# Three sage layers of a graph network put into one block, with the own products issued two tiles ahead

## The chip, the cores and the metric

One Trainium2 chip, one core. The metric is the device time of one execution in microseconds. The kernel before: 2948.05 us, the median of 3 runs (2944.01 to 2951.98).

## What is computed

A stack of four graph layers over 10000 nodes of 512 features and 2500 edges sorted by target, with a pre-norm and a residual around each. The change touches the second one, three "sage" steps in a row (h starts as the layer norm of x, with a relu):

```python
for l in range(3):
    h_neigh = segment_sum(h[src], dst) / maximum(deg, 1)
    rst = h @ W_self[l] + h_neigh @ W_neigh[l] + b[l]
    rst = relu(rst)
    h = rst / maximum(sqrt(sum(rst * rst, axis=-1)), 1e-12)
x = x + h
```

## The kernel before, in words

Nodes live in 79 tiles of 128 rows (NT). They are permuted so that every node which receives an edge lies in the last 20 tiles, the **zone**, tiles 59 to 78 (FT = 59, ET = 20). A sage layer so has an own product (h @ W_self) for every tile, and a neighbour product for the zone's alone. Each f32 product is made of three f16 products of high and low halves: `product` (L211) issues 4 chunks x 3 = 12 matmuls of 128x512. The halves of h, transposed, stay in SBUF (`slots16`) and are overwritten tile by tile with those of the next layer.

`gnn_program` calls `sage_layer(l)` (L1342) three times (L2542). Each call opens a block of its own: five instruction streams that all end before the next block's begin. Weights (`w`, 1 MB), bias and neighbour weights (`wn`) are loaded at the block's start (L1417 to L1419); TensorE and VectorE wait for weights and bias together (`s_w` at 32, L1582 and L1490).

Within a block every engine runs `pipeline` (L87): for step t = 0, 1, ... it emits the listed stages in order, each for tile t - lag; stages named in `edges` for edge tile t - lag. Steps below 12 and from 48 on are written out, those between are a hardware loop over four tiles. The engine streams are in order, so a wait holds all that stands behind it.

TensorE (L1604): `project` (L1584) does the own product of tile t into one of four PSUM banks `ps_z` (waiting for `s_r`, so that the bank of tile t-4 has been read) and, in the zone, the neighbour product on top of it, from `aT`, once `sums.s_lo` says that the edge tile's halves are there. In layer 2 `turn` (L1599) follows with lag 4: it transposes the normalised rows `h3` into one of two banks `ps_t`, waits for `s_turned` (h3 of that tile written) and for `s_lo` >= v.t - 1 (the low half of tile v-2 taken out of the same bank). Last comes `edge_sums`, lag FT - 2: eight 128x128 f32 matmuls of gathered rows and a selection matrix (L1316).

VectorE: `z_sum` (L1492, instruction at L1500) takes z out of PSUM, scaled and with the bias; `length` (L1508) the sum of squares, `clamp` (L1515) its lower bound; `lo_rows` (L1526) or in layer 2 `lo` (L1520) the low half; `residual` (L1533), `stats` (L719) and `aggregate` (L727) belong to layer 2's norm. Edge work: `sums.add` (L1254, L1259), `sums.lo` (L1338), and in layer 0 `sums.moments`. The order in layer 2 (L1541): residual(t-2), z_sum(t), edge_add, stats(t-2), length(t), lo(t-5), clamp(t), aggregate(t-2), edge_lo.

GpSimd: `factor` (L1461), the power -0.5; the norm's factors (L733 to L741); `gather` (L1292), an indirect DMA of an edge tile's source rows into one of two buffers `m`, lag FT - 3, once `sums.lo` has freed the buffer. ScalarE: `unit_rows` (L1571), `hi_rows` (L1559) or `hi` (L1552), `normed` (L1561, instruction at L746), `edge_hi` (L1332), in layer 0 also the norm of the gathered rows (L746). `normed` writes one of two buffers `h3` and waits until the store of tile v-2 has landed.

SP issues the DMAs: `edge_load` first (lag FT - 3: selection matrix L1281 once the sum of edge e-2 is done, carry weights L1240 once its `add` is), then in layers 0 and 1 `store` (L1435, lag 2) and the DMA transpose `turn` (L1439, lag 3); in layer 2 `store_x2` (L1430, lag 3), `store` (L1435, lag 5), `load_x` (L1425, lag 1).

```python
    def turn(v):
        pe.wait_ge(s_turned, v.t + 1)
        wait_count(pe, s_lo, v.t - 1)
...
    def normed(v):
...
        wait_count(act, s_turn, v.t + 1 - nh)
        wait_count(act, h_out[b], 16 * v.uses(nh))
```

Of the kernel before, what the change touches and what calls it, by code (L numbers as in the profile page):

```python
# [5 lines left out]
P = 128  # L6
# [10 lines left out]
C = D // P  # L17
# [32 lines left out]
LOOP_END = 48  # L50

# [58 lines left out]
def gnn_program(nc, x, src, dst, edge_attr, Wc, bc, Wlin, blin, Wself, Wneigh, bsage, W1, b1, W2, b2,  # L110
# [1115 lines left out]

    class Carry:


        def __init__(self, ctx, phase, n=2):  # L1230
            self.n = n
            self.w0 = [sb(ctx, f"{phase}_w0{b}", [P, P]) for b in range(n)]
            self.on = [sb(ctx, f"{phase}_on{b}", [P, C]) for b in range(2)]
            self.s_zero, self.s_added, self.s_on = sems(phase, "zero added on")
            self.w0_in = pair(phase, "w0in", n)

        def load(self, sp, t, kind):
            b = t.buf(self.n)
            wait_count(sp, self.s_added, t.t + 1 - self.n)
# [3 lines left out]
        def clear(self, dve, *others):  # L1243
            for ap in others:
                nc.vector.memset(ap, 0.0)
            nc.vector.memset(self.on[1][:, :], 0.0).then_inc(self.s_zero, 1)
# [15 lines left out]
    class EdgeSums:  # L1262


        def __init__(self, ctx, phase, source, kind, scale, nm, aT, ps_a, normed=False, nsel=2):
            self.source, self.kind, self.scale, self.aT, self.ps_a = source, kind, scale, aT, ps_a
            self.nm, self.nsel = nm, nsel
            self.m = [sb(ctx, f"{phase}_m{b}", [P, D]) for b in range(nm)]
            self.sl = [sb(ctx, f"{phase}_sel{b}", [P, P]) for b in range(nsel)]
            self.s_sum, self.s_hi, self.s_lo = sems(phase, "sum ahi alo")  # L1270
            self.m_in, self.sel_in = pair(phase, "min", nm), pair(phase, "selin", nsel)
            self.carry = Carry(ctx, f"{phase}_carry", nsel)
# [3 lines left out]
        def load(self, sp, e):  # L1276
            b = e.buf(self.nsel)
            if e.t < self.nsel:
                sp.wait_ge(self.carry.s_zero, 1)
# [6 lines left out]
        def clear(self, dve, *halves):  # L1286
            self.carry.clear(dve, *halves, *(sl[0:1, :] for sl in self.sl))
# [19 lines left out]
        def sums(self, pe, e):  # L1307
# [5 lines left out]
            pe.wait_ge(self.sel_in[e.buf(self.nsel)], 16 * (e.uses(self.nsel) + 1))  # L1313
            wait_count(pe, self.carry.s_added, e.t)
# [27 lines left out]
    def sage_layer(l):  # L1342

        final = l == 2
        phase = f"s{l}"
        scale_in = SCALE_LN if l == 0 else SCALE_UNIT
        scale_out = SCALE_LN if final else SCALE_UNIT
        unit = f"self{l}"
        with ExitStack() as ctx:
            w = sb(ctx, f"{phase}_w", [P, 2 * cols[unit]], F16)  # L1350
            wn = sb(ctx, f"{phase}_wn", [P, 2 * cols[unit]], F16)
            bias = sb(ctx, f"{phase}_bias", [P, D])
# [1230 lines left out]
```

## Time and profile before

| | |
|---|---|
| median of 3 runs | 2948.05 us |
| the profiled execution | 2975.29 us |
| its span, first to last instruction | 2973.6 us |
| mean granted clock of TensorE | 0.949 |
| sage layers: first own product to last neighbour product | 614.1 to 1586.7 us |

The profiled execution is 27 us above the median, and 1.7 us of it lie outside of its span. In rows of the trace, a start is in us from the beginning of the span, "x12" counts merged instructions, and "[1.2 <-ACT ...]" is the engine's idle time just before and what ended it. PE is TensorE's matmuls, PEld its weight loads, DVE VectorE, ACT ScalarE, POOL GpSimd, SPq the DMA issues of SP. A 128x512 matmul is shown as 379 ns long but the next starts about 215 ns after it, since they are pipelined.

### The profile page before, as it was taken

The numbers are of one execution on the slowest core, as the hardware profiler recorded it, in microseconds if no ns is written. First come the engines' busy times: TensorE is split into PE (matmuls) and PEld (weight loads), VectorE is DVE, ScalarE is ACT, GpSimd is POOL, SyncE is SP. The second block draws the span as 40 slices with busy tenths as digits, with TensorE's granted clock in tenths as the row PEclk, the third lists the DMA queues.
The fourth block names the chain that finished last, engine by engine and source line by source line (L and its number), as shares of the span: only waits on it lengthen the run. The fifth ranks groups of instructions, "written<-read, shape, count | busy, mean of one in ns | idle before, by whom it ended". The sixth has DMA issues, their size and how long they took to land. (4 is left out here: it accounts for less than half of the span.)

```text
span 2973.6 us, 45046 instructions
## 1 busy us (share of the span) xinstructions
PE 2450.1 (82%) x13328; PEld 1425.9 (48%) x13328; DVE 1950.1 (66%) x4623; ACT 1531.0 (51%) x2250; POOL 1195.6 (40%) x1984
## 2 busy tenths in 40 slices
PE   0146898889887999799997987979999998899964
PEld 0134555434343445344453545756666665344443
DVE  8754788668665886599875444648888888223333
ACT  8144676345333543255433774648888877222270
POOL 3645775426332332255554541104444444001145
PEclk9998999999998999899998998989999999899976
DMA  5063453368765888666654322223333344101177
GB/s 193 19 246 103 146 160 117 105 160 205 147 123 132 203 189 153 154 224 220 198 182 161 100 80 94 82 87 111 126 114 126 128 143 139 48 0 48 50 254 301
DMA packets 379310, 414.16 MB, mean 139 GB/s; under 512 B 198240, under 2 KB 237573, under 8 KB 376206
## 3 DMA queue, kind: packets, MB, share of 16 engines
q1 hardware_dynamic: 350510, 337.43, 38.1%
q0 software_dynamic: 28640, 74.78, 8.6%
q8 instruction: 79, 1.29, 0.2%
q14 instruction: 81, 0.66, 0.1%
HBM read 172.55 MB, written 198.32 MB: 125 GB/s over the span
## 5 line engine op out<-in xcount | busy, mean ns | idle before, releaser
L217 PE MATMUL s_ps_z<-s_w,slots 128*128 128x512 f16 x2844 | 642.9, 383 | 42.1 <-DMA s_bias<-in_L_gnn_b 42.1
L217 PEld LDWEIGHTS s_ps_z<-s_w,slots 128*128 128x128 f16 (+1 forms) x2844 | 280.2, 99 | 361.4 <-DMA s_bias<-in_L_gnn_b 43.3
L1571 ACT ACTIVATE s_g<-s_g,s_rn 128x512 f32<-128x512 f32 x237 | 170.0, 717 | 287.9 <-POOL s_rn L1461 287.9
L1461 POOL TENSOR_TENSOR s_rn<-s_em,minus_half 128x1 f32<-128x1 f32 x237 | 178.5, 753 | 253.1 <-DVE s_em L1515 244.6
L1500 DVE SCALAR_TENSOR_TENSOR s_g<-s_ps_z,s_f,s_bias 128x512 f32<-128x512 f32 x237 | 178.0, 751 | 138.0 <-PE s_ps_z L217 129.7
L2427 PE MATMUL z_ps_z<-slots,z_w 128*128 128x512 f16 (+1 forms) x960 | 212.3, 381 | 8.8 <-DMA z_w<-split_root 8.8
L2294 PE MATMUL u_ps_z<-slots,u_w 128*128 (+2 forms) x1920 | 215.6, 273 | 0.0
L2294 PEld LDWEIGHTS u_ps_z<-slots,u_w 128*128 128x128 f16 x1920 | 187.0, 98 | 22.2
L2396 DVE BATCH_NORM_STATS2 z_stats<-slots 128x6 f32<-128x512 f32 (+1 forms) x76 | 52.2, 687 | 186.7 <-ACT slots L2413 186.7
L1508 DVE SCALAR_TENSOR_TENSOR s_junk<-s_g 128x512 f32<-128x512 f32 x237 | 164.6, 695 | 4.1
L217 PE MATMUL s_ps_z<-s_wn,s_aT 128*128 128x512 f16 x720 | 165.2, 379 | 0.0
L746 ACT ACTIVATE s_h<-s_x,s_norm_sh,s_norm_rs 128x512 f32<-128x512 f32 x79 | 64.2, 813 | 177.5 <-POOL s_norm_sh L741 94.5
L2427 PEld LDWEIGHTS z_ps_z<-slots,z_w 128*128 128x128 f16 x960 | 95.0, 99 | 118.0 <-DMA z_w<-split_root 9.2
L2313 PE MATMUL u_ps_o<-u_w,u_hi 128*128 128x512 f16 x632 | 149.3, 379 | 2.0 <-ACT u_hi L2253 2.0
L2413 ACT ACTIVATE slots<-z_ps_z,bn_cols,z_f 128x512 f32<-128x512 f32 (+1 forms) x76 | 58.7, 772 | 159.3 <-PE z_ps_z L2427 159.2
L1292 POOL DMA_INDIRECT z_m<-h_rows,src_s x20 | 19.0, 950 | 261.8 <-DVE z_aT L1338 256.1
L2232 ACT ACTIVATE u_uT<-u_ps_z,u_minus_b,u_minus_f 128x256 f32<-128x256 f32 (+1 forms) x160 | 80.9, 557 | 76.1 <-PE u_ps_z L2294 68.3
L733 POOL TENSOR_TENSOR u_n_nm<-u_n_mv,minus_one 128x1 f32<-128x1 f32 x79 | 15.0, 190 | 240.6 <-DVE u_n_mv L727 240.6
L217 PEld LDWEIGHTS s_ps_z<-s_wn,s_aT 128*128 128x128 f16 x720 | 70.4, 98 | 85.0
L1526 DVE SCALAR_TENSOR_TENSOR s_halves<-s_g,s_halves 128x512 f16<-128x512 f32 x158 | 108.0, 684 | 2.5 <-ACT s_halves L1559 2.5
L790 ACT ACTIVATE q_h<-slots,q_norm_sh,q_norm_rs 128x512 f32<-128x512 f32 x79 | 60.0, 805 | 96.0 <-POOL q_norm_sh L785 63.4
L217 PE MATMUL e_ps<-e_w,e_hT 128*128 128x512 f16 x480 | 107.1, 379 | 0.0
(393 smaller groups left out, 5684.7 us busy)
## 6 DMA issues: line engine op xcount, KB each, us to landing
h_rows<-s_g SPq DMA_DIRECT2D x158, 256.0 KB
x_rows<-q_x SPq DMA_DIRECT2D x79, 256.0 KB
s_x<-x_rows SPq DMA_DIRECT2D x79, 256.0 KB
x_rows<-s_x SPq DMA_DIRECT2D x79, 256.0 KB
h_rows<-s_h SPq DMA_DIRECT2D x79, 256.0 KB
u_x<-x_rows SPq DMA_DIRECT2D x79, 256.0 KB
x_rows<-u_x SPq DMA_DIRECT2D x79, 256.0 KB
h_rows<-u_h SPq DMA_DIRECT2D x79, 256.0 KB
```

The costliest lines, as they stand in the source:

```text
L217: ins = nc.tensor.matmul(out_ap, a(c), w[:, part * size + c * n:part * size + (c + 1) * n], start=first and c == 0 and m == 0, stop=stop a ...
L746: return nc.scalar.activation(out_ap, in_ap, func, scale=self.rstd[b][:, 0:1], bias=self.shift[b][:, 0:1])
L790: return nc.scalar.activation(out_ap, in_ap, ACT.Relu, scale=self.rstd[b][:, k:k + 1], bias=self.shift[b][:, k:k + 1])
L1461: nc.gpsimd.tensor_tensor(out=rn[b][:, :], in0=em[b][:, :], in1=minus_half[:, :], op=POW).then_inc(s_rn, 1)
L1500: nc.vector.scalar_tensor_tensor(out=g[b][:, :], in0=ps_z[v.buf(4)][:, :], scalar=f[:, 0:1], in1=bias[:, :], op0=MUL, op1=ADD).then_inc(s_ ...
L1508: nc.vector.scalar_tensor_tensor(out=junk[:, :], in0=r[:, :], scalar=0.0, in1=r[:, :], op0=MAX, op1=MUL, accum_out=en[e][:, 0:1]).then_inc ...
L1526: nc.vector.scalar_tensor_tensor(out=part[:, D:2 * D], in0=g[v.buf(ng)][:, :], scalar=scale_out, in1=part[:, 0:D], op0=MUL, op1=SUB).then_ ...
L1571: nc.scalar.activation(g[b][:, :], g[b][:, :], ACT.Relu, scale=rn[v.buf(2)][:, 0:1]).then_inc(s_h, 1)
L2232: ins = nc.scalar.activation(chunk(uT, c, tiles), z_chunk(v, c, tiles), ACT.Sigmoid, scale=minus_f[:, 0:1], bias=minus_b3[:, c:c + 1])
L2294: ins = nc.tensor.matmul(z, w3[:, at:at + P], pair_slots[:, :, part * D + k * P:part * D + (k + 1) * P], start=k == 0 and m == 0, stop=k = ...
L2313: nc.tensor.matmul(ps_o[b][:, :], chunk_of_tile(u_hi, v, c), w4[:, part * cols["out"] + c * D:part * cols["out"] + (c + 1) * D], start=Fal ...
L2427: ins = nc.tensor.matmul(out_ap, weights[:, at:at + P], a(k), start=first and k == 0 and m == 0, stop=stop and k == C - 1 and m == 2)
```

## The change

- `sage_layer(l)` becomes a class `SageLayer` with a method for each engine. `sage_layers()` makes the three layers on shared buffers and opens one block, in which each engine's stream runs layer 0, 1 and 2 one behind the other. What the barriers between the blocks ordered is now ordered by waits on the layer before (`takes_over`).
- The weights of the next layer are loaded once the last own product is done (`s_own`), the bias once the last z has been taken (`s_r` at NT), the neighbour weights once the last product is done. TensorE waits for the weights alone, VectorE for the bias alone.
- TensorE's `project` is split: `own` with lag 0, `neighbours` with lag AHEAD = 2; `edge_sums` gets lag FT - 2 + AHEAD, and layer 2's `turn` lag 5 instead of 4.
- VectorE in layer 2: `lo` stands right behind `z_sum`.
- Three buffers `m` for gathered rows instead of two, and the gather's lag is FT - 4 instead of FT - 3.

```diff
+AHEAD = 2
...
     def gather(self, pool, e):
         b = e.buf(self.nm)
+        if self.like and e.t < self.nm:
+            pool.wait_ge(self.like.s_lo, ET)
         wait_count(pool, self.s_lo, e.t + 1 - self.nm)
...
+    class SageLayer:
...
+            self.sums = EdgeSums(ctx, phase, h_d[l] if l else x1_d, MEAN, self.scale_in, 3, halves, self.ps_a,
+                                 normed=l == 0, like=before.sums if before else None)
...
+        def sync(self, sp, after):
+            def next_weights(v):
+                if after and isinstance(v.t, int) and v.t == NT - 2:
+                    sp.wait_ge(self.s_own, 1)
+                    after.load_weights(sp)
...
+            def load_x(v):
+                b = v.buf(4)
+                if self.takes_over(v, 4):
+                    self.before.rows_turned(sp, b)
...
+            def store(v):
+                b = v.buf(self.nh)
+                if after and isinstance(v.t, int) and v.t == NT - 1:
+                    sp.wait_ge(self.s_r, NT)
+                    after.load_bias(sp)
+                sp.wait_ge(self.s_turned, v.t + 1)
...
+            if self.final:
+                pipeline(sp, NT, (FT - 3, edge_load), (3, store_x2), (5, store), (1, load_x), edges=(edge_load,),
+                         loop_end=LOOP_END)
...
+            else:
+                pipeline(sp, NT, (0, next_weights), (FT - 3, edge_load), (2, store), (3, turn), edges=(edge_load,),
+                         loop_end=LOOP_END)
+                sp.wait_ge(self.s_mm, NT)
+                after.load_neighbour_weights(sp)
...
+        def gpsimd(self, pool):
...
+                pipeline(pool, NT, *node_stages, (FT - 4, edge_gather), edges=(edge_gather,), loop_end=LOOP_END)
...
+        def vector(self, dve):
...
+            dve.wait_ge(self.s_bias, 16)
+            def z_sum(v):
+                b = v.buf(self.ng)
+                dve.wait_ge(self.s_mm, v.t + 1)
+                if self.takes_over(v, self.ng):
+                    dve.wait_ge(self.before.s_lo, last_use(4, b) + 1)
+                    self.before.rows_stored(dve, b)
...
-                    pipeline(dve, NT, (2, residual), (0, z_sum), (FT - 2, edge_add), (2, stats), (0, length), (5, lo),
-                             (0, clamp), (2, lambda v: norm.aggregate(dve, v)), (FT - 2, edge_lo), edges=edges,
-                             loop_end=LOOP_END)
+                pipeline(dve, NT, (2, residual), (0, z_sum), (5, lo), (FT - 2, edge_add), (2, stats), (0, length),
+                         (0, clamp), (2, lambda v: self.norm.aggregate(dve, v)), (FT - 2, edge_lo), edges=edges,
+                         loop_end=LOOP_END)
...
+        def tensor(self, pe):
+            pe.wait_ge(self.s_w, 16)
+            def own(v):
+                zone = in_zone(v)
+                if self.before and isinstance(v.t, int):
+                    if v.t < PEEL:
+                        pe.wait_ge(self.before.turn_out[v.buf(4)], 16 * (v.uses(4) + 1))
...
+                if self.takes_over(v, 4):
+                    pe.wait_ge(self.before.s_r, last_use(4, v.buf(4)) + 1)
+                wait_count(pe, self.s_r, v.t - 3)
+                ins = product(pe, self.ps_z[v.buf(4)][:, :], lambda c: slots16[:, bass.ds(v.t * 2 * D + c * P, P)],
+                              lambda c: slots16[:, bass.ds(v.t * 2 * D + D + c * P, P)], self.w, D, stop=not zone)
+                if not zone:
+                    ins.then_inc(self.s_mm, 1)
+                elif v.t == NT - 1:
+                    ins.then_inc(self.s_own, 1)
+            def neighbours(v):
+                if in_zone(v):
+                    e = tile_of(v.t - FT)
+                    a = self.aT[e.buf(2)]
+                    if e.t == 0:
+                        pe.wait_ge(self.s_wn, 16)
+                    pe.wait_ge(self.sums.s_lo, e.t + 1)
+                    product(pe, self.ps_z[v.buf(4)][:, :], lambda c: a[:, c * P:(c + 1) * P],
+                            lambda c: a[:, D + c * P:D + (c + 1) * P], self.wn, D, first=False).then_inc(self.s_mm, 1)
+            def turn(v):
+                pe.wait_ge(self.s_turned, v.t + 1)
+                wait_count(pe, self.s_lo, v.t - 1)
+                transposes(pe, self.ps_t[v.buf(2)], self.turned[v.buf(self.nh)]).then_inc(self.s_turn, 1)
...
-                turns = ((4, turn),) if final else ()
-                pipeline(pe, NT, (0, project), *turns, (FT - 2, edge_sums), edges=(edge_sums,), loop_end=LOOP_END)
+            turns = ((5, turn),) if self.final else ()
+            pipeline(pe, NT, (0, own), (AHEAD, neighbours), *turns, (FT - 2 + AHEAD, edge_sums), edges=(edge_sums,),
+                     loop_end=LOOP_END)
...
-    for l in range(3):
-        sage_layer(l)
+    sage_layers()
```

## Rows read from the trace of the kernel before

**Rows 1.** The page's first line.
```profile
span 2973.6 us, 45046 instructions
```

**Rows 2.** Busy times by stage; columns as in the first line, stretches in us.
```profile
core 0: us, PE busy (x) PEld busy (x) DVE busy (x) ACT busy (x) POOL busy (x), PEclk, DMA share, GB/s
614.10:766.20 152.10, 152.10 (x696) 68.44 (x696) 128.71 (x284) 75.70 (x112) 72.88 (x78) 0.99 0.79 191
769.50:928.30 158.80, 130.87 (x652) 66.89 (x652) 97.84 (x281) 57.61 (x83) 52.21 (x117) 0.99 0.62 122
...
1100.00:1227.90 127.90, 127.32 (x652) 68.69 (x652) 82.88 (x224) 40.94 (x62) 30.98 (x39) 0.98 0.78 150
1249.40:1448.90 199.50, 182.11 (x900) 87.27 (x898) 186.14 (x501) 104.79 (x163) 114.26 (x278) 1.00 0.63 214
1451.00:1586.70 135.70, 134.75 (x733) 76.47 (x734) 107.01 (x308) 51.63 (x85) 69.04 (x123) 0.99 0.55 181
```

**Rows 3.** Timeline, layer 0's zone: the first sum, and the last two.
```profile
769.50 1.13 PE L1316 MATMUL s_ps_a<-s_sel,s_m 128*128 128x128 f32 x8 [3.27 <-DMA s_sel<-selections]
...
909.21 1.16 PE L1316 MATMUL s_ps_a<-s_sel,s_m 128*128 128x128 f32 x8 [1.27 <-ACT s_m L746]
...
916.82 1.16 PE L1316 MATMUL s_ps_a<-s_sel,s_m 128*128 128x128 f32 x8 [1.27 <-ACT s_m L746]
...
920.72 0.68 DVE L1338 SCALAR_TENSOR_TENSOR s_aT<-s_m,s_aT 128x508 f16<-128x508 f32 x1
```

**Rows 4.** Timeline, layer 2's zone: a sum, normed's start, the store's issue.
```profile
1490.35 1.06 PE L1316 MATMUL s_ps_a<-s_sel,s_m 128*128 128x128 f32 x8
...
1498.60 0.81 ACT L746 ACTIVATE s_h<-s_x,s_norm_sh,s_norm_rs 128x512 f32<-128x512 f32 x1 [3.46 <-DMA h_rows<-s_h]
...
1535.92 1.06 PE L1316 MATMUL s_ps_a<-s_sel,s_m 128*128 128x128 f32 x8
...
1540.44 0.43 SPq L1435 DMA_DIRECT2D h_rows<-s_h  x1
...
1544.94 0.81 ACT L746 ACTIVATE s_h<-s_x,s_norm_sh,s_norm_rs 128x512 f32<-128x512 f32 x1 [4.44 <-DMA h_rows<-s_h]
```

**Rows 5.** Timeline, the seams: between layers 0 and 1, and layer 2's first z.
```profile
930.73 1.23 SPq L1439 DMA_TRANSPOSE slots<-s_halves  x1
...
944.40 17.84 PE L217 MATMUL s_ps_z<-s_w,slots 128*128 128x512 f16 x72 [16.06 <-DMA s_bias<-in_L_gnn_b]
...
949.44 0.75 DVE L1500 SCALAR_TENSOR_TENSOR s_g<-s_ps_z,s_f,s_bias 128x512 f32<-128x512 f32 x1 [10.15 <-PE s_ps_z L217]
...
1249.42 0.75 DVE L1500 SCALAR_TENSOR_TENSOR s_g<-s_ps_z,s_f,s_bias 128x512 f32<-128x512 f32 x1 [10.52 <-PE s_ps_z L217]
```

**Rows 6.** By tile: landing times of the weights, then of the bias.
```profile
DMA to landing us min/median/max: 4.8/4.8/4.9
...
DMA to landing us min/median/max: 6.3/6.3/6.3
```

**Rows 7.** Timeline, layer 1: the first sum and the product behind it.
```profile
1099.99 2.05 PE L1316 MATMUL s_ps_a<-s_sel,s_m 128*128 128x128 f32 x8 [3.08 <-DMA s_sel<-selections]
...
1101.83 4.70 PE L217 MATMUL s_ps_z<-s_w,slots 128*128 128x512 f16 x12
```

**Rows 8.** Timeline, layer 2's end, from the end of its last product.
```profile
1586.67 0.60 PE L228 MATMUL s_ps_t<-ident,s_h 128*128 128x128 f32 x4
...
1586.87 0.75 DVE L1500 SCALAR_TENSOR_TENSOR s_g<-s_ps_z,s_f,s_bias 128x512 f32<-128x512 f32 x1 [2.32 <-PE s_ps_z L217]
...
1588.14 0.68 DVE L1508 SCALAR_TENSOR_TENSOR s_junk<-s_g 128x512 f32<-128x512 f32 x1
...
1588.74 0.69 DVE L1520 SCALAR_TENSOR_TENSOR slots<-s_ps_t,slots 128x512 f16<-128x512 f32 x1
...
1589.57 0.63 PE L228 MATMUL s_ps_t<-ident,s_h 128*128 128x128 f32 x4 [2.30 <-DVE slots L1520]
```

**Rows 9.** Timeline, layer 1: length and clamp with nothing between.
```profile
1228.70 0.70 DVE L1508 SCALAR_TENSOR_TENSOR s_junk<-s_g 128x512 f32<-128x512 f32 x1
...
1229.49 0.15 DVE L1515 TENSOR_SCALAR s_em<-s_en 128x1 f32<-128x1 f32 x1
```

More of the change, by code:

```diff
@@ L1313, in sums @@
             pe.wait_ge(self.sel_in[e.buf(self.nsel)], 16 * (e.uses(self.nsel) + 1))
+            if self.like and e.t == 0:
+                pe.wait_ge(self.like.carry.s_added, ET)
             wait_count(pe, self.carry.s_added, e.t)
@@ new lines, in sage_layers @@
+    def sage_layers():
+        with ExitStack() as ctx:
+            shared = {"w": sb(ctx, "s_w", [P, 2 * cols["self0"]], F16), "wn": sb(ctx, "s_wn", [P, 2 * cols["neigh0"]], F16),
+                      "bias": sb(ctx, "s_bias", [P, D]),
+                      "rows": [sb(ctx, f"s_g{b}", [P, D]) for b in range(4)],
+                      "others": [sb(ctx, f"s_halves{b}", [P, D]) for b in range(4)],
+                      "aT": [sb(ctx, f"s_aT{b}", [P, 2 * D], F16) for b in range(2)],
+                      **{n: [sb(ctx, f"s_{n}{b}", [P, 1]) for b in range(2)] for n in ("en", "em", "rn")},
+                      "ps_z": [ps(ctx, f"s_ps_z{b}") for b in range(4)], "ps_t": [ps(ctx, f"s_ps_t{b}") for b in range(2)],
+                      "ps_a": ps(ctx, "s_ps_a"), "junk": ps(ctx, "s_junk")}
+            layers = []
+            for l in range(3):
+                layers.append(SageLayer(ctx, l, shared, layers[-1] if layers else None))
+            block = ctx.enter_context(nc.Block())
@@ L1474, in _ @@
[L1474 to L1482 removed]
+                for layer in layers:
+                    layer.gpsimd(pool)
@@ L1540, in _ @@
-                if final:
-                    pipeline(dve, NT, (2, residual), (0, z_sum), (FT - 2, edge_add), (2, stats), (0, length), (5, lo),
-                             (0, clamp), (2, lambda v: norm.aggregate(dve, v)), (FT - 2, edge_lo), edges=edges,
-                             loop_end=LOOP_END)
-                else:
-                    pipeline(dve, NT, (0, z_sum), (FT - 2, edge_add), (0, length), (0, clamp), (2, lo_rows),
-                             (FT - 2, edge_lo), (FT - 3, edge_moments), edges=edges, loop_end=LOOP_END)
+                for layer in layers:
+                    layer.vector(dve)
@@ L1573, in _ @@
[L1573 to L1578 removed]
+                for layer in layers:
+                    layer.scalar(act)
             @block.tensor
@@ L1599, in turn @@
-                def turn(v):
-                    pe.wait_ge(s_turned, v.t + 1)
-                    wait_count(pe, s_lo, v.t - 1)
-                    transposes(pe, ps_t[v.buf(2)], turned[v.buf(nh)]).then_inc(s_turn, 1)
-                turns = ((4, turn),) if final else ()
-                pipeline(pe, NT, (0, project), *turns, (FT - 2, edge_sums), edges=(edge_sums,), loop_end=LOOP_END)
+                for layer in layers:
+                    layer.tensor(pe)
     class Mish:
```

438 lines of the change are left out of this document (225 added, 213 removed).

## The prediction

> **What bounds the kernel now.** I read the page first, then the busy times by stage, then the order of time around each seam of the three sage layers. One program fills the span of 2973.6 us [rows 1]; an average over it mixes stages, and each sage layer has two of its own: tiles 0 to 58, then the zone, tiles 59 to 78, in which a tile also takes neighbour products and its edge sums.
>
> In the plain tiles of the first layer TensorE is never idle: 58 products in 152.1 us, 2.6 us each [rows 2]; the second layer's look the same. In the zones the three layers differ [rows 2]. Layer 0: TensorE is busy 131 of 159 us. It waits for ScalarE's normalised gathered rows before each edge sum, one sum every 7.61 us [rows 3]. Layer 1: 127.3 of 127.9 us, so TensorE is the bound. Layer 2: 134.8 of 135.7 us, the bound again, a tile each 6.51 us (45.57 us for seven, from 1490.35 to 1535.92) [rows 4]. The plain tiles of layer 2 are VectorE's: 186 of 199.5 us busy, 3.5 us a tile [rows 2]. Between two layers TensorE is idle for 16.06 us, and its first product then takes 5.04 us instead of 2.6 at the lower clock [rows 5].
>
> **What the change removes.** The sum is made against the profiled execution (span 2973.6 us, its own time 2975.3); the median, 2948.05, is 0.9% lower. I carry the differences over to the median unscaled.
>
> Start of layer 0: TensorE no longer waits for the bias. It landed 6.3 us after its issue, which stood 0.4 us behind that of the weights, and these took 4.8 us [rows 6]: gain 1.9.
>
> Seam 0 to 1: the weights are reissued when the last own product is done, and after that come two neighbour products, an edge sum and a wait, some 9 to 11 us against 4.8 for the landing. Four PSUM buffers let TensorE do own products 0 to 3 (10.3 us) before it needs the first z. That z needs the new bias. SP issues it behind the transpose of tile 76, which stood 2.4 us after TensorE's last product and took 1.2 us to issue [rows 5]; the landing of a DMA is 4.5 to 6.3 us [rows 4, 6]. So z comes 8.2 to 10 us after the last product: hidden, or late by up to 0.5 us. Gain 16.06, plus 2.4 for the slow first product, less 0.3: 18.2. SP also waits in front of the stores and transposes of tiles 75 and 78, for under 1.2 us; their readers come 10 us later.
>
> Seam 1 to 2: the next stage is VectorE's, so what counts is its first z. It came 21.5 us after TensorE's end at 1227.9 [rows 2, 5] and will come 8.2 us after it: 13.3. The second layer's neighbour weights now stand on SP's queue ahead of the first loads of x, which the third z needs; I take off 1.1 (0 to 2). Gain 12.2.
>
> Own products two tiles ahead. In order, TensorE's stream was own(t), neighbour(t), sum; it becomes own(t+2), neighbour(t), sum. The sums keep their place behind the neighbour products, so **layer 0's cycle** (sum, VectorE, moments, GpSimd, ScalarE, sum) stays at 7.61 us. Only its end gets shorter: from the last sum's start to TensorE's end were 11.5 us (916.82 to 928.34); now two neighbour products remain, the last of which waits for the edge's low half at 921.40 and takes 2.6, so 7.2. Gain 4.3 [rows 3, 5]. At the zone's start two own products delay the first sum by up to 1.9 us, and the third gather buffer takes back about as much: 0. **Layer 1**: the idle 3.08 us ahead of the first sum are covered, and with them goes the half clock (sum 2.05 instead of 1.06, product 4.70 instead of 2.6) [rows 4, 7]: 6.2, less 0.9 for the last product's wait: 5.3. The third buffer alone gives nothing in the middle of a zone, where the trace shows no sum of layer 0 or 1 waiting for a gather. A few more semaphore waits and the lost barriers' instructions are put at 0; they run beside TensorE.
>
> Gains together: 1.9 + 18.2 + 12.2 + 4.3 + 5.3 = **41.9** (38 to 45).
>
> **What it adds**, all in layer 2. First, VectorE's low half moves from between length and clamp to right behind z. There it filled the accumulator's read-out: length to next instruction is 0.60 us with it [rows 8], 0.79 us to the clamp without it [rows 9]. 0.19 x 55 tiles = 10.5 on the engine that is the bound; part of it replaces waits for ScalarE that VectorE has already. I take 5 (3 to 11).
>
> Second, the turn. TensorE's step is now own(t), neighbour(t-2), turn(t-5), sum. With u = t-2 it is neighbour(u), turn(u-3). turn(u-3) waits for lo(u-5), since there are two transpose buffers; VectorE does lo(u-5) in its step u, behind z(u), and z(u) waits for neighbour(u), just ahead of the turn. Before, the turn behind neighbour(u) was turn(u-4), whose lo belonged to step u-1. So in each zone tile TensorE now stands from the end of neighbour(u) until z and lo are done: 0.20 + 0.75 + 0.69 + 0.14 = 1.78 us [rows 8]. The cycle is at least 6.51 + 1.78 = 8.29 us.
>
> Third, a **longer loop** closes through SP. turn(u-3) needs ScalarE's normed(u-3), which writes a buffer of two and so waits until store(u-5) has landed. SP issues store(u-5) in its step u, behind the loads of edge u-56, and those wait for the sum of edge u-58. That sum now stands on TensorE directly behind turn(u-4). From a sum's start to the store's issue were 4.52 us, to normed's start 9.02, in the quickest round 8.25 [rows 4]; 18 rounds in the zone show this wait of ScalarE for the store. Before, two TensorE steps (13.0 us) lay over that chain, so it cost nothing; now there is one. The loop: 8.25 to 9.02, normed 0.81, turn to sum 0.44: 9.5 to 10.3 us. I take 9.5, by the quickest round, because with longer rounds SP's queue will be emptier.
>
> The zone is then 18 rounds of 9.5 from the first sum, one of 8.3 (SP has no edge loads left by then) and about 9.9 from the last sum to TensorE's end: 189.2 against 135.7. **Cost 53.5** (32 with the 8.29 us cycle, 68 with 10.3). The tail behind it keeps its order: 0.
>
> For a DMA the Trainium skill (DMA: Bandwidth & Descriptors, Anatomy of one DMA) fits 2.0 us plus the bytes over 436 GB/s, an estimate of 2.6 us for a 256 KB store. The row has 4.50 us from issue to the instruction that waited; by the page's figure the loop would fall under 8.3 us and the whole change would come out near 5 us faster. The measurement decides.
>
> **Sum**: -41.9 + 5 + 53.5 = +16.6 us, 2965.
>
> **The rivals.**
> A, the forecast. Chance 0.55, of its own 2950 to 2990.
> B, the store's loop is shorter than the trace shows, because its transfers were queued behind others; the 8.29 us cycle is left. Cost 31.7: -41.9 + 5 + 31.7 = -5.2, 2943. For it: SP's issues are spread unevenly now. Against: no round in the zone had it under 8.25 us. Chance 0.12.
> C, faster: the turn doesn't stand behind z at all, TensorE stays packed in layer 2's zone (6.51 us). Then only gains and VectorE's 5: -37, 2911. The point is whether normed and lo of the turn's tile are done when neighbour(u) ends; the order in the code says no. Chance 0.08.
> D, as A, and the 3 us of idle time in each round bring the clock down: 3.08 us did so ahead of layer 1's first sum, while layer 0's 1.27 us gaps did not [rows 3, 7]. The slow products are hidden in the loop, the sum and the turn are not: 1.0 + 0.3 us for 18 rounds, +23: 2988. Chance 0.22.
> The Trainium skill (TensorE: Matmul & The Clock Gate, What's actually happening) calls the slower rate the default that activity releases; by that rule D is what gaps of this size invite, and the trace has it both ways, since a 3.27 us gap in layer 0 left the next sum at 1.13 us [rows 3].
> E, the change doesn't do what it says (weights not back in time, the seam keeps most of its idle time): then +40 or more. Chance 0.03.
>
> **Numbers.** The likeliest is 2965. About 0.3% (8.8 us) is what a measurement of this kernel can tell from no change. Faster by more: C and a third of B, 0.12. Within: most of B and the low end of A, 0.19. Slower: 0.69. The range runs from B's 2943 to above D, 2996; it leaves out C, the low end of B, E and the worst of D.
>
> **What would show it.** Right: TensorE idle under 1 us at both seams, first product of layers 1 and 2 at 2.6 us; layer 0's zone at 7.61 us a sum; layer 1's zone without idle time; in layer 2's zone some 3 us of idle TensorE before each turn, released by ScalarE's normed rows, which in turn wait for the DMA of h rows; sums 9.5 us apart. If that idle time is released by VectorE's lo and the sums are 8.3 us apart, B holds. If sums are 6.5 us apart, C, and my reading of the order is wrong. Sums that take 2 us show D. VectorE's plain tiles in layer 2 should take 3.6 us. The forecast fails on one number above all: the 8.25 us from sum to normed.

## The result, and the profile after

**Slower.** The changed kernel takes 2988.43 us (median of 4 runs, 2984.15 to 2994.64), the kernel before 2947.74 beside it (2944.01 to 2951.98): ratio 1.0139, 95% interval 1.0117 to 1.0162, or +40.7 us. The forecast was +16.6 (2965 us) with a range of 2943 to 2996.

The page's first line, and the busy times of the changed kernel by stage: the plain tiles and the zone of layer 0, the zone of layer 1, the plain tiles and the zone of layer 2. They answer to [rows 1, 2].

```profile
span 2982.4 us, 45066 instructions
```
```profile
core 0: us, PE busy (x) PEld busy (x) DVE busy (x) ACT busy (x) POOL busy (x), PEclk, DMA share, GB/s
599.40:752.00 152.60, 152.58 (x695) 68.66 (x696) 128.48 (x283) 75.69 (x112) 73.92 (x79) 0.98 0.81 194
758.50:911.60 153.10, 126.70 (x628) 65.00 (x629) 97.55 (x281) 54.78 (x79) 50.36 (x114) 0.98 0.63 129
1068.50:1189.90 121.40, 119.26 (x628) 65.05 (x629) 82.72 (x224) 39.47 (x60) 30.31 (x38) 1.00 0.80 160
1197.50:1411.00 213.50, 184.58 (x896) 88.43 (x895) 197.63 (x502) 104.06 (x163) 110.52 (x276) 0.98 0.64 210
1416.40:1608.80 192.40, 147.98 (x710) 79.72 (x708) 109.35 (x307) 53.20 (x85) 68.17 (x122) 0.91 0.39 126
```

Read the last two lines against [rows 2]. Layer 2's plain tiles have the same work and take 14 us more, VectorE's busy time among it (186 to 198). Its zone takes 192.4 us instead of 135.7, and TensorE, which had 134.8 busy of 135.7, is now idle for 44 us of it.

The two spans differ by 8.8 us only, although the medians differ by 40.7. The stages that the change doesn't touch ran differently: up to the first weights' issue 607.36 us in the profile of before and 594.52 in this one, behind the layers 1361.0 and 1344.4. So I cut both timelines at the same instructions, VectorE's z of certain tiles, and compare stage by stage:

| stage, us | before | after | change | forecast |
|---|---|---|---|---|
| issue of the first weights to layer 0's last z | 321.0 | 317.3 | -3.7 | -6.2 |
| from there to layer 1's last z | 299.5 | 278.3 | -21.2 | -23.5 |
| from there to layer 2's first z | 21.5 | 7.4 | -14.2 | -12.2 |
| first z to z of tile 57 | 199.5 | 213.5 | +14.0 | +5 |
| z of tile 57 to the last z | 137.9 | 197.9 | +59.9 | +53.5 |
| last z to the next stage's first transposes | 25.8 | 29.2 | +3.4 | 0 |
| sum | 1005.3 | 1043.5 | +38.2 | +16.6 |

The sum of +38.2 agrees with the +40.7 of the medians. The gains are nearly all there (39.1 of 41.9); the costs are 77.3 instead of 58.5. A stage of one profile has some scatter: where two kernels have the same code in a stage, its time differs by up to 2 us (layer 0 takes 315.5 to 317.5 us in the seven profiles of kernels that share the changed kernel's code for it).

**The seams.** TensorE's timeline where layer 0 ends, then VectorE's at both seams, against [rows 5]:

```profile
909.03 2.76 PE L218 MATMUL s_ps_z<-s_wn,s_aT 128*128 128x512 f16 x12 [0.89 <-DVE s_aT L1357]
911.64 43.55 PE L218 MATMUL s_ps_z<-s_w,slots 128*128 128x512 f16 x201
```
```profile
911.84 0.75 DVE L1523 SCALAR_TENSOR_TENSOR s_g<-s_ps_z,s_f,s_bias 128x512 f32<-128x512 f32 x1 [0.62 <-PE s_ps_z L218]
919.30 0.75 DVE L1523 SCALAR_TENSOR_TENSOR s_g<-s_ps_z,s_f,s_bias 128x512 f32<-128x512 f32 x1 [2.40 <-DMA s_bias<-in_L_gnn_b]
...
1197.50 0.75 DVE L1523 SCALAR_TENSOR_TENSOR s_g<-s_ps_z,s_f,s_bias 128x512 f32<-128x512 f32 x1 [2.28 <-DMA s_bias<-in_L_gnn_b]
1204.26 0.69 DVE L1561 TENSOR_TENSOR s_halves<-s_halves,s_g 128x512 f32<-128x512 f32 x1 [3.33 <-DMA s_halves<-x_rows]
```

The first row ends layer 0; the second is layer 1's own products, with no gap and at full clock, where 16.06 us of idle time and a slow product stood. At both seams the bias decides the first z, and behind the second the first residual waits 3.33 us more for its row of x.

**The loop in layer 2's zone.** One round from the timeline, as in [rows 4]: sum, store of h rows, normed rows, turn, next sum.

```profile
1503.64 1.06 PE L1335 MATMUL s_ps_a<-s_sel,s_m 128*128 128x128 f32 x8
...
1506.72 0.43 SPq L1445 DMA_DIRECT2D h_rows<-s_g  x1
...
1507.12 2.75 PE L218 MATMUL s_ps_z<-s_wn,s_aT 128*128 128x512 f16 x12
...
1511.36 0.81 ACT L747 ACTIVATE s_g<-s_halves,s_norm_sh,s_norm_rs 128x512 f32<-128x512 f32 x1 [4.15 <-DMA h_rows<-s_g]
...
1512.22 0.75 PE L229 MATMUL s_ps_t<-ident,s_g 128*128 128x128 f32 x4 [2.35 <-ACT s_g L747]
1512.77 1.92 PE L1335 MATMUL s_ps_a<-s_sel,s_m 128*128 128x128 f32 x8
```

3.08 us to the store's issue, 4.64 to normed's start, 0.86 to the turn, 0.55 to the sum: 9.13 in this round. The 19 steps from the first sum (1416.40) to the last (1596.85) take 180.45 us, 9.50 each on average. The waits of the zone (1416 to 1609), as engine, line, releaser: us in total, times, longest:

```profile
ACT s_g L747 <- DMA h_rows<-s_g: 75.2, 18, 4.5
...
PE s_ps_t L229 <- ACT s_g L747: 43.2, 18, 3.4
```

Before, ScalarE waited as long for the same transfers (78 us in 19 times), and TensorE didn't wait for ScalarE there. The wait is old; what is new is that TensorE stands behind it. It does not end last in every round: of the 20 turns ahead of a sum, three were released by VectorE's low half, after 1.53 us.

### The profile page after: what moved, and what is told of

The parts are those of the page before. It is cut to its first block and busy times, and to the rows that moved or that the text cites. A ratio compares the mean times of both kernels' runs of the same rounds, so it can differ in the third digit from the quotient of the medians.

```text
span 2982.4 us, 45066 instructions
## 1 busy us (share of the span) xinstructions
PE 2471.0 (83%) x13328; PEld 1426.8 (48%) x13328; DVE 1961.2 (66%) x4615; ACT 1531.9 (51%) x2250; POOL 1196.7 (40%) x1984
## 5 line engine op out<-in xcount | busy, mean ns | idle before, releaser
L218 PEld LDWEIGHTS s_ps_z<-s_w,slots 128*128 128x128 f16 (+1 forms) x2844 | 282.0, 99 | 331.7 <-issue 20.7
L747 ACT ACTIVATE s_g<-s_halves,s_norm_sh,s_norm_rs 128x512 f32<-128x512 f32 x79 | 64.2, 813 | 197.6 <-POOL s_norm_sh L742 114.3
L1263 DVE SCALAR_TENSOR_TENSOR s_m<-s_carry_w,s_carry_on,s_ps_a 128x128 f32<-128x128 f32 x240 | 67.4, 343 | 105.0 <-PE s_ps_a L1335 102.4
L734 POOL TENSOR_TENSOR s_norm_nm<-s_norm_mv,minus_one 128x1 f32<-128x1 f32 x79 | 41.1, 520 | 210.5 <-DVE s_norm_mv L728 210.5
L229 PE MATMUL s_ps_t<-ident,s_g 128*128 128x128 f32 x316 | 54.6, 298 | 84.5 <-ACT s_g L747 77.4
```

The costliest lines, as they stand in the source:

```text
L218: ins = nc.tensor.matmul(out_ap, a(c), w[:, part * size + c * n:part * size + (c + 1) * n], start=first and c == 0 and m == 0, stop=stop a ...
L747: return nc.scalar.activation(out_ap, in_ap, func, scale=self.rstd[b][:, 0:1], bias=self.shift[b][:, 0:1])
L1263: ins = nc.vector.scalar_tensor_tensor(out=total[:, c, :], in0=self.w0[w0][:, :], scalar=self.on[1 - b][:, c:c + 1], in1=ps_a[:, c * P:(c ...
```

## The experiments

All ratios are to the kernel before, run beside it. Beside the first four runs it took 2946 us, beside the next four 2975 and beside the last 2969, so microseconds are compared by ratios (0.001 is 2.9 us) and by the stages of the profiles. "All" is from the first weights' issue to the next stage's first transposes, as in the sum above; the last two columns are layer 2's.

| kernel | ratio (95%) | all | first z to z(57) | z(57) to last z |
|---|---|---|---|---|
| before | 1 | 1005.3 | 199.5 | 137.9 |
| changed | 1.0139 (1.0117 to 1.0162) | 1043.5 | 213.5 | 197.9 |
| turn one later | 0.9896 (0.9876 to 0.9916) | 974.5 | 213.2 | 131.2 |
| and low half back | 0.9864 (0.9845 to 0.9882) | 963.9 | 201.8 | 132.0 |
| before, low half moved | 1.0033 (1.0021 to 1.0045) | 1014.2 | 211.0 | 137.5 |
| changed, stores first | 1.0040 (1.0026 to 1.0053) | 1014.9 | 214.6 | 169.3 |
| two gather buffers | 0.9873 (0.9853 to 0.9894) | 966.2 | 202.1 | 135.5 |
| no products ahead | 0.9930 (0.9912 to 0.9947) | 984.6 | 201.9 | 134.3 |
| weights late | 0.9935 (0.9917 to 0.9952) | 990.3 | 199.9 | 131.9 |
| no loop | 0.9842 (0.9822 to 0.9862) | 958.0 | 195.6 | 131.7 |
| neighbour weights later | 0.9847 (0.9830 to 0.9863) | 955.5 | 193.5 | 132.0 |

### The turn one tile later

```
-            turns = ((5, turn),) if self.final else ()
+            turns = ((6, turn),) if self.final else ()
```

> The changed kernel with one edit: in the last layer the turn goes six tiles behind the own product instead of five, so that behind neighbour product u stands turn(u-4) again, whose normalised rows and low half VectorE and ScalarE finish one tile earlier. My theory (the turn's place costs the zone, by a loop sum, edge load, store, normalised rows, turn, sum of 9.5 us): the loop gets a second tile to run in, the sums of layer 2's zone come 6.5 us apart again, and the 56.5 us of the zone, 3.3 of its entry and 3.4 of its tail go: 2988 - 57 to 63 = 2925 to 2931. The plain tiles stay at 3.66 us a tile at the ends and 3.80 in the loop. Rival 1 (the two own products ahead are themselves what stalls: they fill the four accumulators and wait for VectorE's z): sums stay over 7.5 us apart, TensorE waits ahead of its own products, 2950 or more. Rival 2 (only the low half's half of the wait goes, the store loop stays): sums 8.3 to 9.5 us apart, 2965 to 2988.

2917.23 us, 71 less than the changed kernel and 8 below my range; the zone gives back 66.7 us where I had 56.5 and 3.3. TensorE's timeline in the zone:

```profile
1480.89 2.75 PE L218 MATMUL s_ps_z<-s_w,slots 128*128 128x512 f16 x12
1483.48 2.75 PE L218 MATMUL s_ps_z<-s_wn,s_aT 128*128 128x512 f16 x12
1486.07 0.60 PE L229 MATMUL s_ps_t<-ident,s_g 128*128 128x128 f32 x4
1486.51 1.06 PE L1335 MATMUL s_ps_a<-s_sel,s_m 128*128 128x128 f32 x8
1487.40 2.75 PE L218 MATMUL s_ps_z<-s_w,slots 128*128 128x512 f16 x12
```

No wait is left: own product, neighbour product, turn, sum, 6.51 us a round. The own products ahead do not stall, against rival 1; the zone is even 6.7 us shorter than in the kernel before. Most of what made the changed kernel slow is therefore one number, the 5 of the turn's place. The tail keeps its extra 3.5 us (29.3), which I had put down to the turn: here the theory falls. It stands in every run of the new form, between 29.0 and 29.6, the run without products ahead too.

### The low half back in its place

```
-                pipeline(dve, NT, (2, residual), (0, z_sum), (5, lo), (FT - 2, edge_add), (2, stats), (0, length),
+                pipeline(dve, NT, (2, residual), (0, z_sum), (FT - 2, edge_add), (2, stats), (0, length), (5, lo),
```

(on top of the edit above, in VectorE's order of the last layer)

> As the run with the turn six tiles behind, and VectorE's low half of the last layer back between length and clamp. My theory (its place costs 0.25 us a tile over 57 plain tiles, because nothing fills the wait for the accumulator's read-out any more): the plain tiles fall from 3.66 to 3.41 us at the ends and from 3.80 to 3.59 in the loop, the time falls by another 14 us (8 to 16), to 2912 to 2918, some 32 us under the kernel before the change. Rival (the slower plain tiles come from something else in the block, such as GpSimd's or SyncE's order, the low half's place being free): no difference to the other run, plain tiles at 3.66 and 3.80, 2925 to 2931.

2908.79 us, 8.4 less than the last; in the profile the plain tiles take 11.4 less, by the 3.57 us a tile in the loop that the kernel before has too (3.59). So the place of the low half has a price. 14 was too much: 0.25 us a tile is what it costs in the tiles written out, but in the loop a tile falls by 0.23 (3.80 to 3.57), and the first tiles have no low half yet. The wait for x at the seam (3.1 us in the last run, 3.5 in this one) stands in both.

### The kernel before with the low half moved alone

```
-                    pipeline(dve, NT, (2, residual), (0, z_sum), (FT - 2, edge_add), (2, stats), (0, length), (5, lo),
+                    pipeline(dve, NT, (2, residual), (0, z_sum), (5, lo), (FT - 2, edge_add), (2, stats), (0, length),
```

> The kernel before the change with only VectorE's low half moved from between length and clamp to right behind z, in the last layer. My theory: 0.25 us x 57 tiles = +14 us, all in the plain tiles (3.41 to 3.66, 3.59 to 3.80 in the loop), the zone's sums stay 6.51 us apart as TensorE bounds it: 2962 (2956 to 2964), ratio 1.005. Rival 1 (my forecast's own term, mostly hidden behind VectorE's waits for ScalarE): +5, 2953. Rival 2 (the low half earlier frees the turn earlier and the step is not VectorE's): 0 or a gain, 2948 or less.

2958.03 us, +11.7 in the median and +9.7 by the ratio (6 to 13 by its interval), between my 14 and rival 1's 5. The plain tiles of the profile take +11.5, which is nearer to the first, the zone nothing. VectorE's order written out, from the first length to the second's clamp:

```profile
1425.18 0.68 DVE L1508 SCALAR_TENSOR_TENSOR s_junk<-s_g 128x512 f32<-128x512 f32 x1
1425.78 0.14 DVE L1508 DVE_READ_ACCUMULATOR s_junk<-s_g 128x1 f32 x1
1425.96 0.15 DVE L1515 TENSOR_SCALAR s_em<-s_en 128x1 f32<-128x1 f32 x1
...
1426.17 0.69 DVE L1533 TENSOR_TENSOR s_x<-s_x,s_g 128x512 f32<-128x512 f32 x1
1426.97 0.75 DVE L1500 SCALAR_TENSOR_TENSOR s_g<-s_ps_z,s_f,s_bias 128x512 f32<-128x512 f32 x1
1427.64 0.68 DVE L1520 SCALAR_TENSOR_TENSOR slots<-s_ps_t,slots 128x512 f16<-128x512 f32 x1
...
1428.84 0.68 DVE L1508 SCALAR_TENSOR_TENSOR s_junk<-s_g 128x512 f32<-128x512 f32 x1
```

Length to length takes 3.66 us, with no idle time named anywhere in it; in the kernel before it takes 3.41 at this place, and there the low half starts at the same moment as the accumulator's read-out, 0.60 us behind length. Here the read-out stands alone, and the clamp comes 0.78 us behind length (0.79 in [rows 9]).

### The stores ahead of the edge loads

```
-                pipeline(sp, NT, (FT - 3, edge_load), (3, store_x2), (5, store), (1, load_x), edges=(edge_load,),
+                pipeline(sp, NT, (3, store_x2), (5, store), (FT - 3, edge_load), (1, load_x), edges=(edge_load,),
```

> The changed kernel with one edit: on SyncE's queue in the last layer the two stores of a step stand ahead of the edge loads instead of behind them. Nothing moves on TensorE, VectorE or ScalarE. My theory (store(u-5) waits on SyncE for the sum of edge u-58, and so closes the 9.5 us loop): that loop opens, the next shortest is left, neighbour product, z, low half, turn, with 8.3 us a tile, and the turn's idle time is then ended by VectorE's low half instead of ScalarE's normalised rows: 18 x 1.2 = 22 us less and some 3 at the zone's entry, 2963 (2958 to 2968). Rival 1 (the stores are late because their transfers are slow, not because of what stands ahead of them): sums stay 9.5 us apart, 2988. Rival 2 (the edge loads are now late and the sums wait for them): 9 us or more, 2980 or more, with the sums waiting for the selection's or carry's DMA.

2958.92 us, 29.5 less than the changed kernel, with one entry moved on a queue that only issues transfers. The long loop is open, the low half's is left. Two rounds of TensorE and the wait that is left:

```profile
1488.93 0.63 PE L229 MATMUL s_ps_t<-ident,s_g 128*128 128x128 f32 x4 [1.53 <-DVE slots L1547]
...
1497.17 0.63 PE L229 MATMUL s_ps_t<-ident,s_g 128*128 128x128 f32 x4 [1.53 <-DVE slots L1547]
```

The rounds are 8.23 us long, each with 1.53 us of idle time ended by VectorE's low half: the cycle that the forecast had given as 8.29. Both loops of the forecast are thus seen, the store's with 9.50 as the bound of most rounds of the changed kernel, the low half's with 8.23 here, and with the turn one tile later neither.

The edit does two things to the store at once, and rival 1 is not wholly out. The store no longer waits for the sum, and it also lands sooner. Issues with their KB and the median time to landing: the changed kernel's zone, this run's zone, and the changed kernel's plain tiles (1300 to 1380), where no edge loads are issued.

```profile
h_rows<-s_g SPq DMA_DIRECT2D x20, 256.0 KB, 4.4
...
s_carry_w<-selections SPq DMA_DIRECT2D x18, 64.0 KB, 4.1
```
```profile
h_rows<-s_g SPq DMA_DIRECT2D x18, 256.0 KB, 2.6
```
```profile
h_rows<-s_g SPq DMA_DIRECT2D x21, 256.0 KB, 2.2
```

The same store lands after 4.4 us behind the edge loads, of which the carry's broadcast load (64 KB) takes 4.1 itself, and after 2.6 ahead of them. So its transfer is slow in the changed kernel because of what stands ahead of it, and the loop was long on both counts: by the wait on the queue and by some 1.8 us of landing. No run parts the two.

### Two gather buffers

```
-            self.sums = EdgeSums(ctx, phase, h_d[l] if l else x1_d, MEAN, self.scale_in, 3, halves, self.ps_a,
+            self.sums = EdgeSums(ctx, phase, h_d[l] if l else x1_d, MEAN, self.scale_in, 2, halves, self.ps_a,
...
-                pipeline(pool, NT, *node_stages, (FT - 4, edge_gather), edges=(edge_gather,), loop_end=LOOP_END)
+                pipeline(pool, NT, *node_stages, (FT - 3, edge_gather), edges=(edge_gather,), loop_end=LOOP_END)
```

(on top of the run with turn and low half back, as are the next three; layer 0's gathers likewise)

> The run with turn and low half back (2909 us), with two buffers for gathered rows and the gathers one step later, as before the change. My theory (the third buffer is worth nothing in the middle of a zone, where no sum waits for a gather, and little at its start, since the own products two ahead cover the first gather): layers 1 and 2 keep 6.07 and 6.51 us between sums, layer 0 keeps 7.61, 0 to +4 us: 2909 to 2913. Rival (with the products ahead TensorE comes to the sums earlier and now waits for the gathers, so that the third buffer is what lets the first part of the change work): +10 us or more, 2919 or more, with sums released by the DMA into the gathered rows.

Ratio 0.9873 against 0.9864, +2.6 us and inside the intervals; the stages have +2.3. Layer 2's first three steps from sum to sum are 6.67, 7.06 and 6.61 us, all the others 6.51, and its zone takes 3.5 us more; layer 1 takes 1.4 less. The rival's sign is seen once in layer 2, where the first sum waits 3.35 us for its gathered rows; behind it no sum of layers 1 and 2 waits over 0.5 us for a gather. The third buffer is worth 2 us or nothing.

### No own products ahead

```
-AHEAD = 2
+AHEAD = 0
...
-            turns = ((6, turn),) if self.final else ()
+            turns = ((4, turn),) if self.final else ()
```

> The run with turn and low half back (2909 us), with each tile's own product directly ahead of its neighbour product as before the change, in all three layers (and the turn four tiles behind, which is the same place against the neighbour product). The weights' reload and the three gather buffers stay. My theory (the own products ahead are worth 2.0 us at layer 0's end, 2.8 at layer 1's zone, 5.9 at the start of layer 2's zone, and with one neighbour product less behind the last own product the reload no longer fits: up to 5 us at the two seams): +11 to +16, 2920 to 2925. Rival 1 (TensorE bounds the zones whatever the order): 0 to +3, 2909 to 2912. Rival 2 (they are the main gain, the seam is hidden only through them): +20 or more.

Ratio 0.9930: +19.5 us, and 20.7 in the stages; more than I expected, and just short of rival 2. Layer 0 loses 4.6 us, layer 1 9.4, each seam 2.2 and layer 2 2.4. I had missed two things. The end of layer 0 loses 4.1 us, not 2.0, and layer 1's zone 6.3, not 2.8, of which 4.1 are its end: from the last sum to the last z it takes 11.5 us again, as in the kernel before, against 7.4. And the seam costs more than the wait for the weights:

```profile
919.93 2.75 PE L218 MATMUL s_ps_z<-s_wn,s_aT 128*128 128x512 f16 x12
920.13 0.33 SPq L1409 DMA_DIRECT2D s_w<-split_self  x1
...
926.11 9.20 PE L218 MATMUL s_ps_z<-s_w,slots 128*128 128x512 f16 x34 [3.42 <-DMA s_w<-split_self]
```

The weights are issued when the last own product ends, with one neighbour product left in front of them, and TensorE waits 3.42 us for them. The products behind the wait are slow (34 matmuls in 9.20 us, where 12 took 2.75), and layer 1's plain tiles take 3.0 us longer. Of the 5.9 us that I had given to layer 2's zone, 2.3 came. The two parts of the change depend on each other: the products ahead are also what hides the reload.

### The weights late

```
 def next_weights(v):
-    if after and isinstance(v.t, int) and v.t == NT - 2:
-        sp.wait_ge(self.s_own, 1)
-        after.load_weights(sp)
+    return
...
 sp.wait_ge(self.s_mm, NT)
+after.load_weights(sp)
 after.load_neighbour_weights(sp)
```

> The run with turn and low half back (2909 us), with the next layer's own weights loaded only when the last neighbour product is done, instead of when the last own product is. One block, bias, buffers stay. My theory: each seam gets TensorE's wait for the landing, some 5 us by the 4.9 from issue to first product at the start of layer 0, and a first product at half clock, 2.4: +7.5 at seam 0 to 1; at seam 1 to 2 VectorE waits for the bias and x in any case, so only 0 to 5 of it shows: +7 to +13, 2916 to 2922. So of the 16 and 14 us that the two seams gained, less than half is the early reload and the rest the missing end and start of a block (transposes and stores landed, bias behind them). Rival (the early reload is the whole gain): +25 to +30, 2934 or more.

Ratio 0.9935, +21 us, and +26.4 in the stages: my number was wrong, the rival's 25 nearly right. From z to z the seams take 18.0 and 17.8 us instead of 7.6 and 7.4, and layer 1's plain tiles 4.8 us more. The timeline shows why:

```profile
917.82 3.17 SPq L1448 DMA_TRANSPOSE slots<-s_halves  x2
...
921.04 0.58 SPq L1409 DMA_DIRECT2D s_w<-split_self  x1
...
926.23 1.03 PE L218 MATMUL s_ps_z<-s_w,slots 128*128 128x512 f16 x2 [13.19 <-DMA s_w<-split_self]
```

I had counted the landing (5.2 us here) and not the queue. The load stands behind the last two transposes on SyncE and goes out 8 us after TensorE's end (some 913.0). So the early reload carries most of what the seams gained.

### The last layer without its loop

```
-                     loop_end=LOOP_END)
+                     loop_end=PEEL if self.final else LOOP_END)
```

(in the last layer's pipelines on all five engines)

> The run with turn and low half back (2909 us), with the 36 tiles of the last layer that are a hardware loop of four written out. The order of every engine stays. In the loop a tile takes 3.57 us against 3.41 in the tiles written out behind it, the excess standing once in four tiles. My theory (the jump of the loop and what its engines fetch behind it cost VectorE 0.16 us a tile): 3.41 us a tile throughout, 0.16 x 36 = 6 us less, 2903. Rival 1 (the written-out code has to be fetched and costs more): 2909 or more. Rival 2 (the excess is a wait of the four-buffer pattern, not of the loop): no difference.

Ratio 0.9842, 6.4 us under the run with turn and low half back, with intervals that overlap; the profile decides: the plain tiles go from 201.8 to 195.6. My theory holds: the loop's 36 tiles cost 0.17 us each more than written out, and each of them now takes 3.41. What in the jump takes the time is open.

### The neighbour weights later

```
-sp.wait_ge(self.s_mm, NT)
-after.load_neighbour_weights(sp)
+def wait_wn(v):
+    if self.before and isinstance(v.t, int) and v.t == 8:
+        sp.wait_ge(self.before.s_mm, NT)
+        self.load_neighbour_weights(sp)
```

(on top of the last; the new stage stands behind the others of a step on SyncE, in layers 1 and 2)

> The run without the last layer's loop (ratio 0.9842 to the kernel before, measured beside it), with the neighbour weights of layers 1 and 2 issued in the layer's tile 8 instead of ahead of its first loads. In the runs so far the first residual sum of layer 2 waits 3.3 to 3.5 us for its row of x, whose load stands behind these weights. My theory (the 2.3 us by which the plain tiles of the last layer, first z to z of tile 57, stay above the 199.5 us of before, when the low half is back in its place, are this wait): about 2.3 us less from first z to z(57), some 193 us against 195.6 without it, ratio 0.983 to 0.984; nothing lost in layer 1, whose zone needs them 140 us later. Rival (x waits for its own landing, with or without the weights ahead of it): the wait stays over 3 us and the ratio at 0.984; it would be slower if the stores and loads of tile 8 were delayed enough to reach TensorE.

Ratio 0.9847 against 0.9842, which can't be told apart by the runs. In the profile first z to z(57) is 193.5 against 195.6, and the first residual has no wait any more. Predicted 2.3, measured 2.1, but as a difference of two: the wait that is gone was 3.2 us, and at 1231.34 ScalarE now waits 2.63 us for a store behind the moved weights, so that one tile takes 4.39 us instead of 3.41.

## Why the prediction was right or wrong

The direction and the range held, the size did not: +16.6 forecast, +40.7 measured. By the table of stages the forecast is 21.6 us short: 9.0 in layer 2's plain tiles, 6.4 in its zone, 3.4 in the tail, 2.5 in layer 0 and 2.3 in layer 1, less 2.0 at the second seam. The step that failed is a term of the sum, the 5 us for VectorE's low half; the mechanism of the zone, the largest cost, was right.

**Start of layer 0, right.** 594.52 for the issue to 599.42 for the first product, 4.90 instead of 6.74: gain 1.84, forecast 1.9.

**Seam 0 to 1 and layer 1, right by 2 us in 23.** TensorE has no gap, the bias lands 3.8 us after its issue at 915.48, and z(0) comes 7.7 us after the last product (forecast 8.2 to 10). The zone of layer 1 does not run wholly without idle time: it keeps 1.35 and 1.19 us ahead of its first two sums, and 0.89 ahead of the last product.

**Seam 1 to 2, right.** -14.2 against -12.2. That x would be late behind the neighbour weights was right in kind, but mis-sized: the first residual waits 3.33 us for it against my 1.1, and this falls into the next stage of the table. Moving the weights gave 2.1 us back.

**Layer 0's zone, half right.** The end is as forecast (last sum to TensorE's end 7.24, forecast 7.2). But 2.3 us are lost at the zone's start, which I had put at 0: the last sum starts 304.98 us behind the layer's first product (599.42 to 904.40) instead of 302.72. The first sum comes 3.7 us later, where I had allowed 1.9, and the steps behind it give only 1.5 back. The second sum still waits for its normalised rows, 3.86 us where it was 4.97. In the six other profiles with the same code for layer 0 the loss is 0.5 to 1.2 us five times and 2.2 once, so part of the 2.3 is scatter:

```profile
758.54 1.13 PE L1335 MATMUL s_ps_a<-s_sel,s_m 128*128 128x128 f32 x8 [0.95 <-DMA s_sel<-selections]
759.50 2.75 PE L218 MATMUL s_ps_z<-s_w,slots 128*128 128x512 f16 x12
766.12 2.07 PE L1335 MATMUL s_ps_a<-s_sel,s_m 128*128 128x128 f32 x8 [3.86 <-ACT s_m L747]
```

**VectorE's order in the plain tiles, wrong in size.** This is the step that failed: "0.19 x 55 tiles = 10.5 on the engine that is the bound; part of it replaces waits for ScalarE that VectorE has already. I take 5". Measured are 11.5 in the kernel before alone, and 11.4 between the runs with the turn one tile later. The per-tile price was a little low (0.25 where written out, 0.21 in the loop), and the discount was wrong. VectorE's waits for ScalarE were 6.5 us in all in these tiles; with the low half moved 4.3 us of waits are left at the same instruction, so that only 2.2 us of the added time fell into them. Of a tile's 3.59 us in the loop, 3.41 are instructions one behind the other, and most of the rest goes with the loop, as the run without it shows. The other 2.5 us of this stage's +14.0 are the late x at the seam.

**The zone, right in mechanism, its 9.5 partly by luck.** 9.5 us a sum was forecast, 9.50 came, through the store as described, and the run with the stores first takes the loop away. But the number on which the forecast was to stand or fall, 8.25 us from a sum to normed, is 7.75 on average in the twelve rounds with a fast sum; that the average round is 9.50 all the same is in part the slow rounds (below). In the table's terms the low half's loop costs 31.4 us (169.3 less 137.9; forecast 31.7) and the store's loop 28.6 on top of it (197.9 less 169.3; forecast 21.8). The 59.9 against 53.5 is mostly at the two ends. I started the sum with the first edge sum, but its loop bites before. In SyncE's timeline the issues of the broadcast loads of the carried column, which mostly take 0.33 us inside this zone, take 1.85 and 3.60 at its start:

```profile
1400.43 1.85 SPq L1247 DMA_DIRECT2D s_carry_w<-selections  x1
1402.38 1.38 SPq L1437 DMA_DIRECT2D x_rows<-s_halves  x1
1403.80 0.43 SPq L1445 DMA_DIRECT2D h_rows<-s_g  x1
...
1405.16 3.60 SPq L1247 DMA_DIRECT2D s_carry_w<-selections  x1
1408.80 0.42 SPq L1437 DMA_DIRECT2D x_rows<-s_halves  x1
```

The stores behind them are late, ScalarE waits 4.77 us for the store, and the first sum comes 5.4 us after z(57) instead of 2.1: 3.3 us. Of the other 3, 2.1 are the end (11.95 us from the last sum to TensorE's end, forecast 9.9), with a neighbour product at half clock behind 3.36 us of idle time (4.44 us at 1604.35), and 1.1 the rounds. In the kernel before these issues took 1.50 and 3.28 us too, and no turn there waited over 0.97 us for the normed rows; with the turn one tile later the first sum comes 0.3 us ahead of z(57).

**The tail, put at 0, was +3.4**, and 3.2 to 3.8 in the other kernels of the new form against the profile of before. The traces show where: from the end of the last low half to the next stage's first DMA issue it takes 1.54 us in both kernels of the old form (1599.64 to 1601.18 before) and 4.70 to 4.73 in all nine of the new (1621.84 to 1626.56 in the changed kernel). The layers' own work is over by then, so 3.2 of the 3.4 us lie at the end of the one large block. What takes them there was not tried and stays open.

**The rivals.** B (the 8.29 us cycle alone) is what the run with the stores first shows, not this kernel. C's packed TensorE, 6.51 us a tile, is the run with the turn one tile later. D came in part: six of the 20 sums take 1.8 to 1.9 us instead of 1.06, the granted clock of the zone is 0.91 where [rows 2] had 0.99. The Trainium skill (TensorE: Matmul & The Clock Gate, What's actually happening) calls the slow rate the default that activity releases; the trace agrees as far as that goes. The six rounds behind a slow sum average 10.17 us, the other 13 average 9.19 (the last, without edge loads, among them): D's share is by this comparison 6 x 0.98 = 5.9 us of its 23. So the 9.50 is 9.19 by the loop and 0.31 by the clock, where the forecast had 9.5 by the loop alone.

The Trainium skill (DMA: Bandwidth & Descriptors, Anatomy of one DMA) gives its fit for transfers that GpSimd issues; by it a store of 256 KB takes 2.6 us as an estimate, and this store is SyncE's. In the loop's round above the trace has 4.64 from issue to the instruction that waited (4.50 in the kernel before), and with 2.6 this round would have been 7.1 us, under the 8.23 of the low half's loop, and the long loop not the bound. With the stores ahead of the edge loads the median is 2.6 and in the plain tiles 2.2. So the reading "its transfers were queued behind others", which the forecast gave to rival B, was true of the store's time, and it stayed true in the changed kernel.

## What to carry to other kernels

Before a stage is moved by one tile on one engine, write down the tile distances of every loop through it, the DMA queue's order included: the same waits cost nothing with two tiles over them and 60 us with one, about half of it through the low half's loop and half through the store's. Ask of a landing time in such a loop what was issued just ahead of it. A change of several parts is worth taking apart before it is dropped: with the turn's lag at 6 and the low half back, this one is 1.4% faster than the kernel before, and with the last layer's loop written out 1.6%. On an engine that is packed, charge an added gap nearly in full, and find out what its idle time is made of before calling it slack.

## What the runs showed of the hardware

- Pauses of TensorE of 1.53 us in each 8.23 left all 20 sums at 1.06 us (granted clock 0.99 in that zone). With pauses of 1.5 to 3.4 us in rounds of 9.5, six of 20 were slow. Which pause does it is not settled by these rows: in the kernel with the 8.23 us rounds a turn at 1423.03 waited 3.37 us, and its sum was fast.
- A hardware loop of four tiles had one step of 3.95 us and one of 3.53 among steps of 3.41 on VectorE; written out, all 36 tiles took 3.41, 6.2 us less in the plain tiles.
- The issue of one small broadcast load (64 KB) held SyncE's queue for 0.33 us in most rounds of the changed kernel's zone and for 3.60 at its start, with nothing changed in the instruction. In the kernel before it took 0.33 to 1.81 in the zone and 3.28 at its start.
- A 256 KB store landed 2.2 us after its issue (median) in the plain tiles, 2.6 in a zone where it was issued ahead of the broadcast load, and 4.4 where it was issued behind it.
